# Four stacked attention layers on one core: another order of all steps, a shorter cut of the maxima, and key-stack ones set by GpSimd and ScalarE

## What is computed

```python
# block 0: a transformer decoder layer
x = layernorm(x + attention(x, x, mask_self));  x = layernorm(x + attention(ctx, x, mask_cross))
x = layernorm(x + relu(x @ W1.T + b1) @ W2.T + b2)
# block 1: cross attention with normed query and context
qn, cn = layernorm(x), layernorm(ctx);  x = qn + attention(cn, qn) @ wo.T + bo
# block 2: one key/value head, a band of 128 keys, a gate
a = attention_banded(ctx, x) @ Wo + bo;  g = silu(concat(a, x) @ Wg + bg)
y = rms_norm(a * g + x * (1 - g));  x = y - mean_over_tokens(y)
# block 3: pre-norm cross attention and an MLP
x = x + attention(layernorm(ctx), layernorm(x));  x = x + gelu(layernorm(x) @ w1 + b1) @ w2 + b2
```

## Time and profile before

| what | value |
|---|---|
| median of 3 runs | 2636.02 us (2631.29 to 2638.97) |
| the profiled execution | 2635.18 us, span 2633.4 us |
| instructions in the trace | 49,701 |
| mean granted clock of TensorE | 0.975 of 2.4 GHz |
| TensorE busy | 2410.2 us, 92% of the span |
| VectorE, ScalarE, GpSimd busy | 1590.7, 1121.1, 542.3 us |

### The profile page before, as it was taken

The page is one execution under the profiler, slowest core; times in us unless marked ns, Lnnn a source line. Parts: engine busy times, 40 slices in busy tenths (PEclk is TensorE's granted clock), DMA queues, the critical chain, the costliest instruction groups (busy, mean ns, idle before and its releaser), DMA issues.

```text
span 2633.4 us, 49701 instructions
## 1 busy us (share of the span) xinstructions
PE 2410.2 (92%) x18862; PEld 1749.2 (66%) x18862; DVE 1590.7 (60%) x2676; ACT 1121.1 (43%) x1762; POOL 542.3 (21%) x1278
## 2 busy tenths in 40 slices
PE   6999989999998898999989899999999999998976
PEld 4676766667676675766757567676767676676654
DVE  7756566665656557466574754766665757567432
ACT  1344345453444434535344344444444534544422
POOL 3221112222212132221112321111222212212110
PEclk8999999999999899999999999999999999999986
DMA  6412122231221122212111221211322221121100
GB/s 214 115 50 56 34 56 78 58 88 49 62 54 42 38 78 75 66 38 58 45 54 50 79 79 42 62 42 42 83 67 77 61 60 38 38 79 38 37 21 17
DMA packets 164235, 159.15 MB, mean 60 GB/s; under 512 B 17824, under 2 KB 162720, under 8 KB 162976
## 3 DMA queue, kind: packets, MB, share of 16 engines
q1 hardware_dynamic: 164000, 155.97, 21.6%
HBM read 35.71 MB, written 4.19 MB: 15 GB/s over the span
## 4 chain that ended last, share of the span: by engine, by line
PE 56%; issue 22%; DVE 8%; ACT 4%; POOL 3%; POOLq 2%; DVEq 2%; DMA 1%; SPq 1%; ACTq 0%
PE work L1067 13%; PE work L1058 11%; PE out L1148 6%; PE unit L1126 6%; PE unit L1100 5%; DVE neg_max L943 4%; PE unit L1096 4%; PE unit L1122 3%; ACT probs L726 2%; PE work L1049 2%; PE work L1263 2%; POOLq L669 1%; POOL resid L605 1%; DMA query_stack<-max_rows 1%; POOLq L666 1%
## 5 line engine op out<-in xcount | busy, mean ns | idle before, releaser
L943 DVE TENSOR_REDUCE neg_max<-unit 128x4 f32<-128x1024 f32 (+1 forms) x640 | 728.8, 1165 | 335.3 <-PE unit L1100 328.9
L726 ACT ACTIVATE probs<-unit 128x1024 f32<-128x1024 f32 (+1 forms) x640 | 609.1, 980 | 527.6 <-PE unit L1126 525.5
L1067 PE MATMUL work<-par,hidden_t 128*128 128x256 f32 x1792 | 417.9, 383 | 9.4 <-ACT hidden_t L681 6.0
L1100 PE MATMUL unit<-key_stack,query_stack 96*128 96x256 bf16 x2048 | 356.4, 280 | 35.4 <-DVE neg_max L943 17.9
L1067 PEld LDWEIGHTS work<-par,hidden_t 128*128 128x128 f32 x1792 | 332.4, 190 | 63.1 <-ACT hidden_t L681 9.7
L1126 PE MATMUL unit<-query_stack,key_stack 99*128 99x256 bf16 x2048 | 350.0, 277 | 25.6 <-ACT probs L726 9.2
L1058 PE MATMUL work<-tok_t,par 128*128 128x256 f32 x1408 | 339.0, 389 | 7.6 <-ACT tok_t L681 5.1
L1100 PEld LDWEIGHTS unit<-key_stack,query_stack 96*128 96x128 bf16 x2048 | 193.6, 100 | 162.4 <-DVE neg_max L943 38.6
L1058 PEld LDWEIGHTS work<-tok_t,par 128*128 128x128 f32 x1408 | 262.3, 194 | 49.6 <-ACT tok_t L681 9.9
L1148 PE MATMUL out<-probs,values 128*17 128x256 f32 x4096 | 269.6, 383 | 2.1 <-ACT probs L726 1.9
L1126 PEld LDWEIGHTS unit<-query_stack,key_stack 99*128 99x128 bf16 x2048 | 193.4, 99 | 90.0 <-ACT probs L726 19.4
(11 more groups left out here) (162 smaller groups left out, 3408.7 us busy)
## 6 DMA issues: line engine op xcount, KB each, us to landing
query_stack<-query_pieces SPq DMA_DIRECT2D x480, 128.0 KB, 2.4
key_stack<-key_pieces SPq DMA_DIRECT2D x384, 128.0 KB, 2.4
c_in<-in_ctx SPq DMA_DIRECT2D x16, 256.0 KB, 2.9
tok_t<-in_x_features SPq DMA_DIRECT2D x16, 256.0 KB, 2.8
ctx_t<-in_ctx_features SPq DMA_DIRECT2D x16, 256.0 KB, 3.0
x_in<-in_x SPq DMA_DIRECT2D x16, 256.0 KB, 3.1
m_in<-in_mask_self SPq DMA_DIRECT2D x16, 256.0 KB, 3.4
par<-in_params SPq DMA_DIRECT2D x4, 1024.0 KB, 6.3
```

Source lines behind the costliest of these rows:

```text
L726: a_.activation(probs[:, n % PROB_BUFS, :, :, 0:width(l)], bank[:, :, :, 0:width(l)], ACT.Exp, scale=SCALE[l]).then_inc(exped, 1)
L943: v.tensor_reduce(neg_max[:, n % HALVES, :, 2 * (u % 4):2 * (u % 4) + 2], bank[:, :, :, 0:width(l)], AX.X, ALU.max, negate=True).then_inc( ...
L1067: last = pe.matmul(bank[:, t, :], src[:, t * P:(t + 1) * P], weight, start=(n == 0), stop=(n == len(parts) - 1))
L1100: last = pe.matmul(bank[:, t, i, 0:n], queries[0:ROWS, h, t * P:(t + 1) * P], keys[0:ROWS, 0 if l == "l2" else h, columns(l, t)], start=ma ...
```

## The change

Five things change.

1. `CHAIN`, `BESIDE`, `SETUP_STEPS` and `ORDER` are replaced. They hold the same 3,461 steps in another order.
2. `pieces0` and `pieces1` on GpSimd use four small instructions in place of five: the third piece is written by the second subtraction itself, in bf16. A drain follows.
3. The ones of key stacks 0 and 2 are set by GpSimd (a memset each, before it waits for `zeroed`), those of stack 1 by ScalarE (a broadcast copy after `zeroed`). VectorE no longer sets them.
4. TensorE waits for `stack_ones` before the first `exp0` on each of the three stacks.
5. At three steps GpSimd waits for the group of weights of the one bias it uses, no longer for three groups.

Counted from the two lists (TensorE steps are those in which TensorE has work):

| in the order | before | after |
|---|---|---|
| three score steps in a row on TensorE | 135 | 59 |
| ... of them all three `max` | 40 | 17 |
| at most 3 TensorE steps between the last maximum of a half and its `turn` | 28 | 25 |
| at most 3 TensorE steps between `turn` and its first `exp` | 36 | 10 |
| TensorE steps from `q` to `max0`, median | 10 | 11 |
| `max4` ahead of `pieces0` (of 80 layers) | 64 | 16 |
| a `max` right behind a split or norm on VectorE | 99 | 91 |
| two splits or norms next to each other on VectorE | 48 | 56 |
| `qsplit` at most two places behind the `weigh3` that frees its stack | 8 | 19 |

The first steps of the new order are: the loads of sequence 0 (features of x first), `par0`, `par1`, `self.ksplit`, `self.inputs`, `fold`, `self.q`, `self.qsplit`, `self.loadm2`, `self.ctxln`, the next load, `l2.keys`, `l2.ksplit`, `self.negc`, two loads of sequence 1 around `wo_self`, `self.ctxlnb`, `par4`, `wo_cross`, `self.max0`. Before it: `par0` second, `fold`, `par5`, `self.ctxln`, `par1`, `par7`, `self.inputs`, `self.ksplit`, `self.q`, `self.qsplit`, `wo_self`, `wo_cross`, `turn_wo`, `columns_l1`, `l2.keys`, `l2.ksplit`, `self.max0`.

The diff, with the lists cut:

```diff
--- before.py
+++ after.py
@@ -82,27 +82,27 @@
 MIXES = 4
 
 CHAIN = (
-    "self.loadxt self.ksplit self.q self.qsplit self.max0 self.max2 self.max1 self.max3 self.max4 self.pieces0 "
-    "self.max6 self.max7 self.turn0 self.max5 self.pieces1 self.exp0 self.exp1 self.turn1 self.exp3 self.exp2 "
-    "self.weigh0 self.exp4 self.exp5 self.weigh1 self.exp6 self.exp7 self.weigh2 self.weigh3 self.out0 self.out1 "
...
+    "self.loadxt self.ksplit self.q self.qsplit self.max0 self.max3 self.max2 self.max1 self.pieces0 self.max4 "
+    "self.max6 self.turn0 self.max7 self.max5 self.pieces1 self.exp0 self.exp3 self.turn1 self.exp1 self.exp2 "
+    "self.weigh0 self.exp4 self.weigh1 self.exp5 self.exp6 self.exp7 self.weigh2 self.weigh3 self.out0 self.out1 "
...
 )
 BESIDE = (
-    "self.loadc self.loadct self.loadx self.loadm self.ctxln self.inputs self.loadm2 l2.keys l2.ksplit self.negc "
+    "self.loadc self.loadct self.loadx self.loadm self.inputs self.loadm2 self.ctxln l2.keys l2.ksplit self.negc "
     "self.ctxlnb self.ctxnT cross.ksplit l1.keys l1.ksplit l3.keys l3.ksplit "
 )
 
@@ -117,45 +117,45 @@
 
 
 SETUP_STEPS = (
-    "par0 fold par5 par1 par7 wo_self wo_cross turn_wo columns_l1 par6 par4 columns_l3 par2 row_l1 row_l3 row_l2 "
-    "turn_bo par3 bg wg par8 "
+    "par0 par1 fold wo_self par4 wo_cross columns_l1 par5 par6 turn_wo par8 par7 row_l2 par3 columns_l3 par2 row_l1 "
+    "row_l3 turn_bo bg wg "
 ).split()
 ORDER = (
...
 )
 LANES = "0123456789abcdefABCDEFGHIJKLMNOPs"
 
@@ -359,6 +359,7 @@
         loaded = [sem(f"loaded{i}") for i in range(len(GROUPS))]
         folded = sem("folded")
         zeroed = sem("zeroed")
+        stack_ones = [sem(f"stack_ones{s}") for s in range(KEY_STACKS)]
         band_ready = sem("band_ready")
 
         def attention_before(numbers, key, n):
@@ -581,6 +582,14 @@
             for t in range(T):
                 g.tensor_copy(neg_band[:, t, :], band[:, t, columns("l2", t)])
             g.memset(mean_w[:], 1.0 / S).then_inc(band_ready, 1)
+
+            def ones_in_stack(n):
+                g.drain()
+                g.memset(key_stack[n][ROWS:P, :, :], 1.0).then_inc(stack_ones[n], 1)
+                g.drain()
+
+            ones_in_stack(0)
+            ones_in_stack(2)
             pool.wait_ge(setup_loaded, 48)
             pool.wait_ge(zeroed, 1)
 
@@ -634,10 +643,11 @@
                         spread(values[s], c_in[b % CONTEXTS]).then_inc(spread_done, 1)
                     elif (l, step) in (("self", "lnT"), ("cross", "lnT"), ("cross", "lnqT")):
                         wait_full_work(pool, key)
-                        wait_loaded(pool, b, "bo_cross", "l0_b2", "bo_l1")
+                        bias = {("self", "lnT"): "bo_cross", ("cross", "lnT"): "l0_b2", ("cross", "lnqT"): "bo_l1"}[l, step]
+                        wait_loaded(pool, b, bias)
                         if step == "lnqT":
                             wait_folded(pool, b, "row_l1")
-                        with_bias(resid[s], resid[s], {"lnqT": "bo_l1"}.get(step, {"self": "bo_cross", "cross": "l0_b2"}[l]))
+                        with_bias(resid[s], resid[s], bias)
                     elif (l, step) == ("l2", "proj"):
                         wait_taken(pool, key)
                         g.tensor_tensor(quarter(b, l, 1), quarter(b, l, 0), summed[s][:], ALU.subtract).then_inc(diff_ready, 1)
@@ -659,15 +669,15 @@
 
                             wait_full_work(pool, tuple(PIECES_NO.earlier(key, HALVES)[:2])
                                            + ("turn" + PIECES_NO.earlier(key, HALVES)[2][-1],))
-                        for piece in range(3):
-                            src = neg_max[:, half] if piece == 0 else max_rest[:]
-                            last = g.tensor_copy(max_pieces[:, n % HALVES, :, HC * piece:HC * (piece + 1)], src)
-                            if piece < 2:
-                                g.drain()
-                                g.tensor_tensor(max_rest[:], src, max_pieces[:, n % HALVES, :, HC * piece:HC * (piece + 1)],
-                                                ALU.subtract)
-                                g.drain()
-                        last.then_inc(max_cut, 1)
+                        piece = [max_pieces[:, n % HALVES, :, HC * k:HC * (k + 1)] for k in range(3)]
+                        g.tensor_copy(piece[0], neg_max[:, half])
+                        g.drain()
+                        g.tensor_tensor(max_rest[:], neg_max[:, half], piece[0], ALU.subtract)
+                        g.drain()
+                        g.tensor_copy(piece[1], max_rest[:])
+                        g.drain()
+                        g.tensor_tensor(piece[2], max_rest[:], piece[1], ALU.subtract).then_inc(max_cut, 1)
+                        g.drain()
 
             run(SCHEDULE)
 
@@ -675,6 +685,9 @@
         @block.scalar
         def _(act):
             a_ = nc.scalar
+
+            act.wait_ge(zeroed, 1)
+            a_.copy(key_stack[1][ROWS:P, :, :], ones[ROWS:P, 0:1].unsqueeze(2).broadcast_to((P - ROWS, H, S))).then_inc(stack_ones[1], 1)
 
             def take(key, dst):
                 bank, taken = wait_full_work(act, key)
@@ -783,8 +796,6 @@
                 v.memset(out_psum[a][:], 0.0)
             v.memset(max_pieces[:], 0.0)
             v.memset(ones, 1.0)
-            for s in range(KEY_STACKS):
-                v.memset(key_stack[s][ROWS:P, :, :], 1.0)
             v.drain()
             dve.sem_inc(zeroed, 1)
 
@@ -1106,6 +1117,8 @@
 
                 b, l, step = key
                 u = int(step[3:])
+                if u == 0 and l != "l2" and KEY_NO.place[b, l, "ksplit"] < KEY_STACKS:
+                    pe.wait_ge(stack_ones[KEY_NO.place[b, l, "ksplit"]], 1)
                 if u % 4 == 0:
                     n = TURN_NO.place[b, l, f"turn{u // 4}"]
                     pe.wait_ge(max_placed[n % 2], 16 * (n // 2 + 1))
```

More of the change, by code:

```diff
@@ L84 @@
 CHAIN = (
[3 rows of a table removed]
-    "self.mix0 self.values self.mix1 self.outT self.proj self.ln self.lnb self.lnT cross.q cross.qsplit cross.max0 "
[3 rows of a table removed]
-    "cross.outT cross.proj cross.ln cross.lnb cross.lnT cross.hid1 cross.hid2 cross.hid3 cross.hid0 cross.hid_out "
[10 rows of a table removed]
[3 rows of a table added]
+    "self.values self.mix1 self.mix0 self.outT self.proj self.ln self.lnb self.lnT cross.q cross.qsplit cross.max0 "
[14 rows of a table added]
 )
 BESIDE = (
-    "self.loadc self.loadct self.loadx self.loadm self.ctxln self.inputs self.loadm2 l2.keys l2.ksplit self.negc "
+    "self.loadc self.loadct self.loadx self.loadm self.inputs self.loadm2 self.ctxln l2.keys l2.ksplit self.negc "
     "self.ctxlnb self.ctxnT cross.ksplit l1.keys l1.ksplit l3.keys l3.ksplit "
@@ L156 @@
[L156 to L158 removed]
+    "0AAAAss0As00AA1AAABsBABss00A000B21000B10001ss0B000B0B11B0s010B00sBA010001010sB0C0111010C110s111C01s0"
+    "C1200ss11s11210C0112000s0101s000s10210C1021022101B000102002122012000C102C2C202022202110C122201001101"
@@ new lines @@
+    "1000220110221210D110A001121A111201101110s1112C121012011s20120C0210C110002122001020010200001001100022"
+    "2020120222BB2D22121222AA22220212122120211021012110110212101211122D0021120111220111010001010201000210"
+    "2012020110200C020C002010111110110122012B2B112012011D111211201200112212201022121020222212122221220010"
+    "20200020020021010002020100001201022210002022210221102200022222220E22022212021101211032111231233DD12D"
+    "211011321112E3C131C12113111323331313221333131133D22D3DEE1323321D2212231201233D4224232442D32123E32323"
@@ new lines @@
+    "4223EE443234FE4322E2442E424342334442E44424E12F324444243233444E4F24433423433332443533F424344335333333"
+    "434334434344F43544453443334444534DD43355F44534325554F4445554534355334355545553553F43F54455F55F54553F"
+    "35433544455335335F3354334343E35E343H3333533455455545553345355355355344354E455E45534G5444354453453545"
+    "444453454445545344443533454334543334543453335335444F54434G443334335544F43344543445344544344444344455"
+    "3454555454535455345454354554D43D555533554454G4535444344344534454444543543343354443333443453433433353"
@@ new lines @@
+    "53G3433344334335H3535453433354443557553535G53G366555455G6657555366G3G567565H557GH4556566656H566H65H6"
+    "566H6767H5667755767F5FH66577757666576H776677H77G6757H7775755775775775575575555575567757765I5565655G5"
+    "776777757577757667757GI77755I777I757577767I65567667656766675686866568666786H76H766766686686878768876"
+    "86768887I8J766888677667786I77688867686688GG88677678767888I7777I77I6I767788576786668877776687I676I678"
+    "6768687666GG676676668686788878867887J87788868886878688776778687677788867867877787786686I86867I776886"
@@ new lines @@
+    "787768777878766768768788768676868H6867H667766687K668666888678688878876688888778687777668887768776787"
+    "J876786877787877777686766867668668K6687686676766766788676668J87666886688867886888686877867666J7K6997"
+    "998JJ88J88J889888J89KK9K89989989K899986899a98I8I8988999Ja9699988a8989a89K888K898J989898a89KKaa9J8888"
```

(10 more changed lines are left out.)

40 lines of the change are left out of this document (5 added, 35 removed), and 27 rows, old and new, of the table CHAIN.

## The result

| kernel | median | ratio to before, 95% interval |
|---|---|---|
| before | 2636.66 us | |
| changed | 2493.46 us (2490.34 to 2498.73) | 0.946, 0.9442 to 0.9477 |

The account below looks back on a forecast made before the run. TensorE, busy 2410.2 of 2633.4 us, was taken as the bound, so only idle and low-clock time could be won. Terms -6 -15 -5 -4 +7 -3 -3 sum to -29 us, from 2635.2 to 2606 us, range 2573 to 2637.

Parts of the forecast that it names:

- spread thinly over transposes and projections: TensorE's remaining waits, beyond those on maxima, exponentials, pieces and turned maxima; given no term in the sum.
- spacing: Score steps on TensorE wait less for maxima and exponentials as runs of three fall from 135 to 59: -15 us.
- pieces: TensorE's waits for GpSimd's pieces of the maxima shrink with one instruction fewer in the chain: -4 us, bounds +3 and -9.
- turned maxima: Waits for the small transfer between turn and first exp shrink as close places fall from 36 to 10: -5 us.
- start: Moving the ones off VectorE and loading keys earlier brings the first scores sooner: net -6 us, bounds -12 and 0.
- bunches: Maxima queued behind long VectorE steps, splits or norms, make one more long TensorE gap: +7 us, bounds -14 and +21.
- the clock: Time at TensorE's lower clock that the other terms give back: -3 us of about 25, bounds 0 and -10.
- three signs: Forecast wrong if score-step waits stay at 52 us, gaps over 2 us become more frequent, or middle clock drops to 0.98.
- rival (c): At the start, VectorE steps wait out GpSimd's fills on shared SBUF ports: +4 us on the forecast, 2610 us, chance 0.08.
- (a): Spacing is worth all of its 29 us, pieces their 6.5, and no extra bunch comes: 2582 us, chance 0.22.
- (b): Stalls move: TensorE waits at the next producer, and only start and pieces gain: 2629 us, chance 0.12.
- (d): Eight added pairs of long VectorE steps become long gaps at 7 us each: slower, 2655 us, chance 0.08.

Follow-up runs that it names:

- e5: Changed kernel with 72 swaps of neighbouring TensorE steps that bring runs of three score steps from 59 back to 135: 2571.58 us.
- e7: Kernel before with 56 swaps of neighbouring TensorE steps that bring runs of three score steps from 135 down to 74: 2644.83 us.
- e2: Changed kernel with the old lists of steps, so the code changes without the new order: 2625.56 us.
- e1: Kernel before with the new lists of steps and nothing else, so the order alone: 2509.29 us.
- e4: Kernel before with only the ones of the key stacks moved from VectorE to GpSimd and ScalarE: 2628.27 us.
- e15: Changed kernel with two loads of weights, par4 and par5, issued later, behind the first exponentials: 2494.93 us.
- e9: Kernel before with 76 swaps of neighbouring TensorE steps that keep runs of three score steps at 135, first draw: ratio 1.0114, +31.5 us.
- e16: Changed kernel with 76 swaps of neighbouring TensorE steps that keep runs of three score steps at 59, second draw: ratio 0.9591, +34.7 us.
- e17: Kernel before with 76 swaps of neighbouring TensorE steps that keep runs of three score steps at 135, second draw: ratio 1.0128, +33.2 us.
- e13: Kernel before with VectorE's maxima taken over a quarter of the keys and the exponential's scale at 1e-24: 2566.45 us.
- e14: Changed kernel with VectorE's maxima taken over a quarter of the keys and the exponential's scale at 1e-24: 2466.99 us.

## Why the prediction was wrong

It named the direction, not the size: 2606 us for 2493. The step that failed is the costing of the waits, and above all two terms at nothing: the waits "spread thinly over transposes and projections", and busy time, which was to stay since "its work is the same". The span fell by 141.2 us. In the view that the forecast was made from, the matmuls' own:

| part | forecast | measured |
|---|---|---|
| spacing: the five rows of score steps | -15 | -31.9 |
| pieces | -4 | -11.0 |
| turned maxima, the one row | -5 | -4.5 |
| start: waits for `zeroed` and the folded weights | -6 | -7.0 |
| products into `work`, on ScalarE or VectorE | nothing | -29.1 |
| all other idle time | +7 (bunches), -3 (splits) | -11.0 |
| busy time of the matmuls | nothing (-3 by the clock) | -46.7 |

By its steps:

- **"The rest is spread thinly over transposes and projections."** Costed at nothing, with no reason given. These waits gave -29.1 us here and -31.7 at the weight loads (78.7 to 47.0). Spread thinly was true, and is no reason for the change to pass them by: a new order of all steps touches every pair.
- **"What bounds the kernel now."** "TensorE's idle time (223 us) and the time it works at a low clock" was large enough as a bound. The error was to price waits from it: matmul waits leave out what hides under the matmul before. The weight loads have waits of 518 us where the matmuls show idle time of 223, and 46.7 us of the gain came out of busy time (forecast 2390 to 2410 us, measured 2363.5). None of the three signs by which I was to know that I was wrong appeared; this one did.
- **"Spacing of the score steps", -15.** Right in kind, half the size: -31.9 in its own rows (inside the bound of -43), -50.8 at the weight loads. The forecast took half of 29 us because the long waits had another cause, and that rested on one wait of 3.02 us. The triples as a measure hold in part: 0.44 us each or somewhat more when put in (e5), about 0.2 when taken out (e7). At most 33 of the 143 us can be laid to their 76 by the price of e5, 43 with the other draw.
- **"Turned maxima", -5, and pieces, -4.** The first was right, -4.5. The pieces' wait fell by 11.0 us, beyond the bound of -9. At the weight loads it is -10.1, where the code alone takes 9.8 (24.8 to 15.0, e2) and the order alone adds 8.2 (33.0, e1).
- **"VectorE's bunches", +7.** Wrong in sign. Gaps of TensorE over 2 us between 50 us and the last 84 fell from five (3.02, 2.61, 2.54, 2.52, 2.03) to one (2.67). The count of adjacent long steps said nothing of what waits behind them.
- **The clock, -3.** Too small. Outside the first 50 us and the end, the rows of windows and the mean clocks leave some 67 us at the lower level before and 33 after. At most 17 us came back by it, against a bound of 10. "The clock over the middle stays at 0.99" was true only as rounded.
- **"The start", -6.** First scores at 25.23 us against a forecast of 24 to 28, query product 13.87 against 15, key cast 9.57 against 11.5: this chain was right. The fill on ScalarE took 3.60 us (5.0 taken), on GpSimd 3.51 (4.2 taken). But at 50 us little is left in the table of windows, as exp0 waits at 42 us; the ones alone are worth 6 us (e4).
- **The port lock, rival (c).** Two of VectorE's steps for the keys were slow: the cast at 10.99 us, beside a fill, took 1.14 us in place of 0.43, and the subtraction at 12.23, beside GpSimd's copy, 1.05 in place of 0.69. That is 1.1 us, not 4. Waits of this kind show; the price didn't decide anything.
- **Splits and SyncE, -3.** No run and no row separates this term.
- **Rivals.** (a) went the right way and stopped at 2582 us; it too was priced from the matmuls' waits. (b), the stalls move, held for e15 alone. (d), slower, had no place in the trace.

The low end of the range, 2573, left room for 63 us. It was built of bounds from the same rows, and those rows hold 47 us of the gain.

What stays open: which property of an order makes it better, since neither triples nor one kind of wait accounts for it; whether the old order was the looser one (e9, e16, e17); what "issue" hides where the matmul view has no gap; and what of ScalarE's, DMA's and VectorE's other work makes up the 99.5 us of e13 and e14, which the traces divide by class of wait but no run separates.

## What to carry to other kernels

Where TensorE bounds a kernel, read the waits of its weight loads beside those of its matmuls, which hide the first part of each: their listed waits (518 us here, of which 141 went) are what an order can win, the gaps too short to be listed stayed. Such an order is a matter of hundreds of waits of a few tenths of a microsecond, so give a price to the class that is spread thinly too. A count of one pattern prices a small part of it. Before a run with swaps is read, a control with as many neutral swaps is needed, as they cost 0.4 to 0.6 us each here. A single stall near the start can be a stop for a load that is due next anyway, as in e15: see what waits there before you move it.

## What the runs showed of the hardware

The same 18,862 matmuls were busy for 2410.2 us in one order and 2363.5 in the other, with means that hardly moved (L1100 280 ns, now 276), at mean granted clocks of 0.975 and 0.983.

Each of the five gaps of over 2 us in the middle of the kernel before had the clock at its lower level by 2 us after its end, as had the one in the changed kernel. The first ended at 213.78 us, the third at 1181.05, that of the changed kernel at 795.53 (windows as in the earlier trace rows, the clock third from the end of a row):

```profile
215.00:218.00 3.00, 2.83 (x11) 2.18 (x11) 1.70 (x2) 2.40 (x4) 1.24 (x2) 0.50 0.37 98
...
1181.00:1190.00 9.00, 8.24 (x39) 5.70 (x40) 7.00 (x9) 3.13 (x5) 1.09 (x6) 0.50 0.25 68
```

```profile
797.00:800.00 3.00, 3.00 (x8) 2.40 (x8) 1.55 (x6) 1.66 (x2) 0.88 (x2) 0.50 0.01 3
```

The lower level also came without such a gap, in the changed kernel from 1258 to 1261 us for one.

A fill of 32 x 4096 bf16 elements took 3.47 us on VectorE, 3.51 on GpSimd and 3.60 on ScalarE, from a broadcast. Of VectorE's steps beside a GpSimd fill, the cast from fp32 to bf16 took 1.14 us in place of 0.43, while the subtraction ahead of it, beside the same fill, took its usual 0.69.
